# Block-sparse query and key rows: one product each and a spread by transfers, instead of one product for each place

## What is computed

```python
q = jax.nn.relu(jnp.einsum('btd,nde->btne', x, encoder_query))   # 8 heads of 16
v = jax.nn.relu(jnp.einsum('btd,nde->btne', x, encoder_value))
...                              # metric: softplus of a small network on the mean of q
for h in range(NH):
    kw = q_h[:, idx, :]                       # the 64 tokens up to this one
    diff = kw - q_h[:, :, None, :]
    dist = jnp.sqrt((diff * diff * metric).sum(-1) + 1e-08)
    neg, loc = jax.lax.top_k(-dist, k_act)    # 32 nearest
    infl = jnp.exp(-topd) / sum
    context = sum over the nearest of infl * v, plus a gated term of q_h
    outs.append(q_h * context)
```

## Time and profile before

| | |
|---|---|
| median of 3 runs | 2972.43 us (2961.26 to 2973.3) |
| the profiled execution | 2964.93 us, span of its instructions 2963.2 us |
| granted TensorE clock, mean | 0.921 of full speed |
| instructions | 60847 |
| DMA | 84.79 MB, mean 29 GB/s |

### The profile page before, as it was taken

One profiled execution on the slowest core, in us unless ns is written; L12 is line 12 of the kernel. 1 busy time (PEld: TensorE's weight loads), 2 busy tenths in 40 slices (PEclk: granted clock), 3 DMA queues, 4 the chain that ended last, 5 costly groups with the idle time before them and its releaser, 6 DMA issues.

```text
span 2963.2 us, 60847 instructions
## 1 busy us (share of the span) xinstructions
PE 2411.7 (81%) x21171; PEld 1048.0 (35%) x21171; DVE 2112.0 (71%) x10282; ACT 2263.2 (76%) x3151; POOL 688.7 (23%) x869
## 2 busy tenths in 40 slices
PE   4788778888788887988888897888888888887666
PEld 1112242244332443334432443324433344224444
DVE  5801778957797668966789577876689667982695
ACT  4798668977699677987689776996779877994432
POOL 3020115111251114401152112511134011311331
PEclk6599789999899999999889998999999999999887
DMA  3011001100011001210011000110012000000000
GB/s 87 30 46 43 2 19 48 50 18 6 23 56 43 17 8 28 65 31 9 20 44 54 18 6 23 54 42 17 6 35 65 31 9 12 14 17 1 17 20 11
DMA packets 98518, 84.79 MB, mean 29 GB/s; under 512 B 19954, under 2 KB 79540, under 8 KB 98212
## 3 DMA queue, kind: packets, MB, share of 16 engines
q1 hardware_dynamic: 97968, 80.41, 9.2%
q10 hardware_dynamic: 244, 0.49, 0.1%
HBM read 55.32 MB, written 25.44 MB: 27 GB/s over the span
## 4 chain that ended last, share of the span: by engine, by line
ACT 34%; PE 33%; DVE 19%; issue 6%; POOL 5%; SPq 2%; DMA 0%; ACTq 0%; DVEq 0%; POOLq 0%
PE banks L802 30%; ACT PT L1141 17%; DVE xn L1473 4%; ACT pq L1128 4%; DVE h L1476 3%; DVE pq L1260 2%; ACT xn L1086 2%; ACT hparts L1152 2%; POOL Aop L781 2%; PE banks L809 2%; ACT h L1153 2%; ACT h L1054 1%; DVE h L1458 1%; ACT Bs L1054 1%; POOL qkf L728 1%
## 5 line engine op out<-in xcount | busy, mean ns | idle before, releaser
L1141 ACT ACTIVATE PT<-banks 128x1024 f32<-128x1024 f32 x1024 | 996.6, 1038 | 47.4 <-PE banks L802 44.7
L1260 DVE CUSTOM_DVE_ANT_0 pq<-pq,banks 128x512 f32<-128x512 f32 x1024 | 653.4, 683 | 175.5 <-ACT pq L1128 174.8
L1128 ACT ACTIVATE pq<-banks 128x1024 f32<-128x1024 f32 x512 | 523.2, 1023 | 223.5 <-PE banks L802 198.1
L802 PE MATMUL banks<-PT,Vg 128*9 128x512 f32 x4096 | 545.9, 605 | 2.3 <-ACT PT L1141 2.3
L802 PE MATMUL banks<-Q,K 51*128 51x512 bf16 x2048 | 391.0, 393 | 139.9 <-ACT PT L1141 113.3
L802 PE MATMUL banks<-K,Q 48*128 48x512 bf16 x2048 | 360.9, 431 | 80.6 <-ACT pq L1128 37.2
L762 POOL TENSOR_TENSOR hparts<-h,hparts 128x512 fp32r<-128x512 f32 x112 | 140.5, 1272 | 1009.2 <-ACT h L1153 1009.2
L1473 DVE MATCH_REPLACE8 xn<-h,xn 128x96 f32<-128x96 f32 x1536 | 352.2, 241 | 0.0
L802 PE MATMUL banks<-hparts,W 128*128 128x512 f32 x1024 | 303.9, 426 | 39.6 <-ACT h L1153 27.8
L802 PEld LDWEIGHTS banks<-Q,K 51*128 51x128 bf16 x2048 | 96.2, 93 | 620.4 <-ACT PT L1141 534.9
L1476 DVE MAX8 h<-xn 128x8 f32<-128x96 f32 x1536 | 263.0, 243 | 0.0
(11 more groups left out here) (207 smaller groups left out, 3256.3 us busy)
## 6 DMA issues: line engine op xcount, KB each, us to landing
Vw<-scratch_v SPq DMA_DIRECT2D x256, 51.0 KB, 2.1
scratch_k<-pq SPq DMA_DIRECT2D x24, 384.0 KB, 3.1
K<-scratch_k SPq DMA_DIRECT2D x126, 72.0 KB
qkf<-in_hidden_states SPq DMA_DIRECT2D x16, 512.0 KB, 4.4
scratch_q<-pq SPq DMA_DIRECT2D x24, 256.0 KB, 2.3
Q<-scratch_q SPq DMA_DIRECT2D x126, 48.0 KB
K<-scratch_k SPq DMA_DIRECT2D x126, 48.0 KB
scratch_v<-Bs SPq DMA_DIRECT2D x8, 544.0 KB, 3.5
```

The lines of the kernel that those rows point to most:

```text
L802: return pe.matmul(o, l, r, start=start, stop=stop)
L1128: act.activation(cut(g), ring_pair if work is TURN0 and g % 2 else pair[0], ACT.Relu).then_inc(diff_out.sem, 1)
L1141: act.activation(PT[:, at:at + 2, :], pair[g % ESLOTS], ACT.Exp, scale=1.0 if i % 8 < 4 else -1.0).then_inc(probs.sem, 1)
L1260: dve.tensor_tensor_reduce(r, r, pair[1 + g % 2][:, par, :], 1.0, -3.0e38, ALU.subtract, ALU.max, mred[:, par, i, qt:qt + 1]).then_inc(max ...
```

## The change

- eqd and the places' order change: in qd and B the linear copies of four heads fill partitions 0 to 63, the squared copies 64 to 127. The masks half0, half1 and the loads of w2d and rows follow (27 loads instead of 31 at the start).
- "qd" loses its four products. SyncE, once "he" is evicted and the last Aop of the batch before is made, copies qh's 64 rows of each half to both places of qd: four DMAs.
- "key" is two products of xrev with eq into kh (a new name for a part of h2); "pad" is a copy of 64 columns on VectorE; at "spread" SyncE copies kh's rows to B by four DMAs. GpSimd waits for the first four at "aop" 0, VectorE for the others at "keys".
- "qtok" is eight transposes of qh instead of eight products.
- The exponential and logarithm of the metric and VectorE's operations behind them move to "an", and "an" moves behind "qtok".
- xrev is no longer continued by 64 columns.
- The slots and weights of P are new, and since the number of ring uses is now odd, each turn has its own list with its own bank numbers.

The diff, cut to its core:

```diff
-USES = dict(..., he=1, qd=1, hid=1, mod=1, key=1, pad=1, an=1, ...)
+USES = dict(..., he=1, hid=1, mod=1, key=1, an=1, ...)
-WEIGHTS P, from "flip" on: 0.90, 2.00, 2.00, 1.00, 1.31, 1.00, 1.94, 2.00, 2.00, 0.48, 2.00, 2.21, 0.55, 1.10, 1.10, 1.11, 1.11
+WEIGHTS P, from "flip" on: 0.90, 2.00, 1.94, 2.00, 1.00, 1.00, 2.00, 1.00, 2.21, 0.55, 1.10, 1.10, 1.11, 1.11
-SLOTS_P += [(1, [("flip", 0), ("flip", 1)]), (2, [("he", 0), ("he", 1)]), (2, [("qd", 0), ("qd", 1)]), (1, [("hid", 0), ("ev", 0)]),
-            (1, [("qd", 2)]), (1, [("mod", 0)]), (1, [("qd", 3)]), (2, [("key", 0), ("key", 1)]), (2, [("key", 2), ("key", 3)]),
-            (1, [("pad", 0), ("an", 0)]), (2, [("qtok", 0), ("qtok", 1)]), (4, [("keys", 0)]),
-            (1, [("gate", 0)]), (2, [("hebb", 0), ("hebb", 1)]), (2, [("aop", 0)]), (2, [("dist", 0)]), (2, [("dev", 0)])]
+SLOTS_P += [(1, [("flip", 0), ("flip", 1)]), (2, [("he", 0), ("he", 1)]), (1, [("qd", 0)]), (2, [("key", 0), ("key", 1)]),
+            (1, [("spread", 0), ("hid", 0), ("ev", 0)]), (1, [("mod", 0)]), (2, [("qtok", 0), ("qtok", 1)]), (1, [("an", 0)]),
+            (4, [("keys", 0)]), (1, [("gate", 0)]), (2, [("hebb", 0), ("hebb", 1)]), (2, [("aop", 0)]),
+            (2, [("dist", 0)]), (2, [("dev", 0)])]
...
 SyncE
+            def spread(to, rows, sem):
+                for f in range(2):
+                    for half in range(2):
+                        sp.dma_start(to[64 * half:64 * half + 64, f, :], rows[64 * f:64 * f + 64, :]).then_inc(sem.sem, 16)
...
+                    if stage == "qd":
+                        for i in range(2):
+                            sp.wait_ge(*R.moved(c, use["he", i]))
+                        sp.wait_ge(*aop_p.at(b, 0))
+                        spread(qd, qh, qd_in)
+                    if stage == "spread":
+                        for i in range(2):
+                            sp.wait_ge(*R.moved(c, use["key", i]))
+                        sp.wait_ge(*kpad.at(b, 1))
+                        spread(B, kh, b_in)
...
 TensorE
-                    if stage == "qd":
-                        h = n % 2
-                        one(c, k, [(R.bank(k)[:, :], eqd[:, n // 2, :], xT[:, HALF * h:HALF * h + HALF], True, True)])
                     if stage == "key":
-                        h = n % 2
                         if n == 0:
                             pe.wait_ge(*R.made(c, k, use["flip", 0], use["flip", 1]))
-                        one(c, k, [(R.bank(k)[:, :], eqd[:, n // 2, :], xrev[:, HALF * h:HALF * h + HALF], True, True)])
-                    if stage == "pad":
...
+                        one(c, k, [(R.bank(k)[:, :], eq[:, :], xrev[:, HALF * n:HALF * n + HALF], True, True)])
                     if stage == "qtok":
-                        one(c, k, [(R.bank(k)[:, P * q:P * q + P], xT[:, P * (4 * n + q):P * (4 * n + q) + P],
-                                       eq[:, :], True, True) for q in range(4)])
+                        pe.wait_ge(*R.free(c, k))
+                        for q in range(4):
+                            ins = pe.transpose(R.bank(k)[:, P * q:P * q + P], qh[:, P * (4 * n + q):P * (4 * n + q) + P], ident[:, :])
+                        ins.then_inc(R.ready.sem, 1)
...
 ScalarE
-                    if stage == "key" and n == 0:
+                    if stage == "key":
+                        evict(c, k, kh[:, HALF * n:HALF * n + HALF], R.bank(k)[:, :], ACT.Relu)
+                    if stage == "an":
                         act.wait_ge(*met_z.at(b, 1))
                         act.activation(met[:, 3, :], met[:, 2, :], ACT.Exp, scale=-1.0).then_inc(met_e.sem, 1)
                         act.wait_ge(*met_e.at(b, 1))
                         act.activation(met[:, 4, :], met[:, 3, :], ACT.Ln, bias=1.0).then_inc(met_l.sem, 1)
-                    if stage in ("qd", "key"):
...
 VectorE
-                        dve.wait_ge(*R.moved(c, use["flip", 1]))
-                        dve.tensor_copy(xrev[:, T:RPAD], xrev[:, T - 1:T].broadcast_to([P, WIN])).then_inc(xpad.sem, 1)
...
-                    if (stage, n) == ("key", 3):
+                    if stage == "spread":
+                        dve.wait_ge(*R.moved(c, use["key", 1]))
+                        dve.tensor_copy(kh[:, T:RPAD], kh[:, T - 1:T].broadcast_to([P, WIN])).then_inc(kpad.sem, 1)
+                    if stage == "an":
                         dve.wait_ge(*met_l.at(b, 1))
...
-                        dve.wait_ge(*R.moved(c, use["key", 3]))
-                        dve.wait_ge(*R.moved(c, use["pad", 0]))
+                        dve.wait_ge(*b_in.at(b, 1))
                         dve.wait_ge(*v_out.at(b, 2))
```

More of the change, by code:

```diff
@@ L61 @@
 PT_SLOTS = 4
-USES = dict(qk=4, v=1, turn=1, back=1, wo=1, mturn=1, lnT=1, lnTa=2, fa=1, fb=1, fc=1, flip=1, he=1, qd=1, hid=1, mod=1,
-            key=1, pad=1, an=1, qtok=1, hebb=1, dist=2, ev=2, wt=2, pv=1, st=1, dec=1)
+USES = dict(qk=4, v=1, turn=1, back=1, wo=1, mturn=1, lnT=1, lnTa=2, fa=1, fb=1, fc=1, flip=1, he=1, hid=1, mod=1,
+            key=1, an=1, qtok=1, hebb=1, dist=2, ev=2, wt=2, pv=1, st=1, dec=1)
 def uses(stage, n):
@@ L230 @@
 FIRST, FIRST_USE, _k = numbered(HEAD, 0)
-TURN0, TURN0_USE, _k0 = numbered(phases(True, False, False), _k)
-NR = sum(uses(stage, n) for _, stage, n in phases(True, True, True))
-TURN1, TURN1_USE, _k1 = numbered(phases(True, True, False), _k0 - NR)
-TURN, TURN_USE, _ = numbered(phases(True, True, True), _k1 - NR)
-TURN7, TURN7_USE, _k7 = numbered(phases(False, True, True), _k1 - NR)
-LAST, LAST_USE, _ = numbered(TAIL, _k7)
-assert NR % 2 == 0
+TURN0, TURN0_USE, _k = numbered(phases(True, False, False), _k)
+TURN1, TURN1_USE, _k = numbered(phases(True, True, False), _k)
+TURNS = []
+for _c in range(2, NB - 1):
+    _work, _use, _k = numbered(phases(True, True, True), _k)
+    TURNS.append((_work, _use))
+TURN7, TURN7_USE, _k = numbered(phases(False, True, True), _k)
+LAST, LAST_USE, _ = numbered(TAIL, _k)
 class Count:
@@ L254, with __init__ @@
 class Ring:
-    def __init__(self, banks, sem, name, uses):
+    def __init__(self, banks, sem, name):
         self.banks = banks
-        self.ready = Count(sem(f"{name}_ready"), uses)
-        self.evicted = [Count(sem(f"{name}_evicted{i}"), uses // 2) for i in range(2)]
+        self.ready = Count(sem(f"{name}_ready"), 0)
+        self.evicted = [Count(sem(f"{name}_evicted{i}"), 0) for i in range(2)]
     def bank(self, k):
@@ L453, in hybrid_block_kernel @@
         ln_q = count("ln_q", 2)
-        xpad = count("first_repeated", 1)
+        kpad = count("first_key_repeated", 1)
+        qd_in = count("query_rows_spread", 1, 4 * 16)
+        b_in = count("key_rows_spread", 1, 4 * 16)
         met_z = count("metric_in", 1)
@@ L1181, in go @@
                     if stage == "qtok":
[L1182 removed]
+                        evict(c, k, qtok[:, 4 * n:4 * n + 4, :], rows_of(R.bank(k), P))
                     if stage == "gate":
```

40 lines of the change are left out of this document (13 added, 27 removed).

## The result

| | before | after |
|---|---|---|
| median of four runs each | 2968.5 us (2961.3 to 2973.3) | 3001.9 us (2998.8 to 3007.0) |
| ratio, 95% interval | | 1.011 (1.0094 to 1.0126) |
| span of the profiled execution | 2963.2 us | 3005.3 us |
| granted TensorE clock, mean | 0.921 | 0.904 |

The predicted 2973 us is 29 us too low, and the time lies 2 us outside the range. The profiled executions are 42 us apart, the medians 33 us: the one of after is the slowest of its four, the one of before lies 4 us under its median.

What follows compares the result with a forecast made beforehand. No engine full; VectorE's order was taken to decide the stretch from "he" to "dist". Per turn +2.7 - 1.2 = +1.5 us, seven turns +10.5, tail -2.8: +7.7 on 2964.9, forecast 2973 us, range 2933 to 3000.

Steps and rivals of the forecast that it cites:

- rival B: TensorE at its lower clock from "qtok" to "dist", slowing "hebb" and distance products: +2.5 us a turn, 2993 us; chance 0.24.
- The order slides by two groups: New weights put "flip" after 54 row-maximum groups instead of 52, with 8 instead of 10 between "he" and "dist".
- Ahead of "he", +2.7 us: Two more groups ahead of the encoder products: one among the feed-forward products, one ahead of the normalization; +2.7 us a turn.
- Its part for the normalization: One added group behind "fcd", ahead of the normalization on VectorE's full queue: two cut maxima, +1.3 us a turn.
- The part for the feed-forward products: One added group there turns one cut distance of 1.71 us into two of 1.56: +1.4 us a turn.
- The clock, nothing in the sum: TensorE's granted clock from "an" on had no term in the sum; its lower level was left to rival B.
- From "he" to the first distance, -1.2 us: Walk from "he" to the first distance eviction: about 31.9 us instead of 33.1, most of TensorE's saving becoming idle time.
- The metric's wait at "an": TensorE waits for VectorE's metric ahead of the "an" products, 2 to 3 us, no longer covered by key products.
- The transfers, nothing: Query and key row copies, 2.1 MB a batch, cost nothing: covered by 3.7 us or more ahead of "keys".
- Rival C: Rows arrive late: at twice the transfer time +3.5 us a turn and +3 in the tail, 3003 us; chance 0.08.
- The tail, -2.8 us: Tail without groups: "mod" gains 1.1 us, "an" follows two short transposes, so "keys" comes 2.8 us sooner.
- TensorE's busy time, -71 us: Removed "qd", key and "qtok" products take 8.9 us of TensorE a batch, 71 us in all.

Runs made afterwards that it cites:

- e12_one: Kernel before, all products kept, P's weights lowered half way (sum 79.04), so one group more stands ahead of "he": 2981.2 us, 1.0047.
- e2_slide: Kernel before, all products kept, only P's weights lowered (sum 76.65) to give the changed kernel's order up to "he": 2999.6 us, 1.0097.
- e1_order: Changed kernel with P's last weights raised (sum 81.44), restoring the order of before ahead of "he": 2977.1 us, 1.0022.
- e3_busy2: Changed kernel plus six unused 512-column products a batch, two ahead of the "an" wait, four at "gate": 2979.7 us, 1.0033.
- e9_ordmet: Changed kernel with the order of before ahead of "he" and the metric's steps moved from "an" to "qtok": 2960.3 us, 0.9973.
- e4_metric: Changed kernel with the metric's exponential and logarithm moved to the first "qtok", VectorE's operations to the second: 2990.6 us, 1.0071.
- e7_double: Changed kernel with each spread preceded in its queue by the same four transfers into DRAM: 3035.3 us, 1.0225.

## Why the prediction was wrong, step by step

Two terms of the sum failed: the price ahead of "he", which was too low, and the clock from "an" on, which stood in the sum with nothing and was left to rival B.

- *The order slides by two groups: right.* *Ahead of "he", +2.7 us: too low by 1.9 us a turn* (4.55). Its part for the normalization held: +4.9 at "he" in the turn shown less 3.8 at the last "fcd" leaves 1.1 against 1.3. The part for the feed-forward products, +1.4 by the distance of two cuts, measured 3.8. I had priced one added group; e12_one shows 3.6 us without one. In turn 1, without side "q", "he" comes 9.1 us later, and I had given turn 1 the price of the others; e2_slide has 5.8 of it, and the other 3.3 us are open. With the order of before, 25 us of the loss are gone (e1_order).
- *The clock, nothing in the sum: wrong; rival B had the mechanism.* "hebb" takes 3.78 us instead of 2.05 (rival: 3.2), the first distances 1.61 instead of 1.53 (rival: 2.8). With TensorE kept busy by unused products "hebb" is back at 2.05 us and 22 us are gone (e3_busy2). It doesn't take the missing products: e2_slide has them all and the same 3.78 us in every turn. The 25 and the 22 us can't be added up, as the order moves the clock too.
- *From "he" to the first distance, -1.2 us: the size came out on the mean (-1.4; -0.5 in the turn that I had walked through), the reason did not.* e2_slide wins the same 1.4 us with all products in place. What their removal was to give went into the metric's wait and the clock: in the order of before, moving the metric gives 15 to 17 us (e9_ordmet against e1_order).
- *The metric's wait at "an": right.* Forecast 2 to 3 us, measured 2.0. It was in the sum, but as harmless; moved out, it gives 11 us (e4_metric), and 15 to 17 in the order of before (e9_ordmet).
- *The transfers, nothing: right in the turns, with 2.2 us of cover instead of 3.7.* SyncE took 0.8 us for each issue, not 0.4, and they landed in 4.2 and 4.7 us, as the rows below show. In the turn shown the query rows are there 10.1 us behind "he" (forecast 9.5), the key rows at 15.9 (15), the store at 18.0 (18); keys asked at 20.5 instead of 21.7. Rival C at twice the time was priced at 3.5 us a turn; e7_double, with twice the bytes, measured some 3.6 us (355.0 against 351.4) in turns 3 to 6 and 7 us in turn 2.
- *The tail, -2.8 us: wrong, +7.1.* Both its parts failed: keys wait for the store, and the clock stays down for 30.7 us. The tails with all products take 212.4 us (before), 214.0 (e2_slide) and 216.5 (e12_one), so 3 to 7 us belong to the change itself.
- *The exponent stage, nothing: wrong, +1.2 us a turn.*
- *TensorE's busy time, -71 us: wrong, -25.* The products went (76 us); the slower "hebb" and "an" took 22 us back, and other groups 29.

The sum as it came out, where I had 1.5 us for each of seven turns and -2.8: 4.55 - 1.5 + 0.4 + 1.2 = 4.6 us in each of turns 2 to 6 (0.4 between the first distance and the first exponential; the -1.5 is of these five turns), 8.8 in turn 1, 3.6 in turn 7 and 7.1 in the tail: 42 us.

## What to carry to other kernels

Where one list orders all engines, an edit that changes the weights behind a point also moves every step ahead of it: run the kernel before with the new weights alone before you judge the edit, and don't price a shift by counting groups. And look at the clock of the kernel with the new weights as well: here the order alone put "hebb" at the lower level. The products taken off TensorE gave nothing as long as the wait that they had covered stayed (the metric's, 15 to 17 us). With that moved and the order of before, the change pays, though "hebb" still runs at the lower level (29.7 us in e9_ordmet). Taken together, the change with the order of before and the metric made early is 0.3 to 0.4% faster than the kernel before; as it was made it is 1.1% slower.

## What the runs showed of the hardware

DMA issues of the changed kernel by tile, beside the earlier trace rows (count, size of one, us to landing):

```profile
B<-h SPq DMA_DIRECT2D x32, 272.0 KB, 4.7
...
qd<-qh SPq DMA_DIRECT2D x32, 256.0 KB, 4.2
scratch_q<-pq SPq DMA_DIRECT2D x24, 256.0 KB, 2.5
...
scratch_v<-Bs SPq DMA_DIRECT2D x8, 544.0 KB, 5.1
```

256 KB from 64 partitions to 64 land in 4.2 us (the first of each four in 2.9 to 3.1), where the 256 KB stores to DRAM that were there before (scratch_q) take 2.5; the store behind them takes 5.1 us instead of 3.5. The Trainium skill's page "SBUF — State Buffer", "Door 1: The DMA port swizzle", has 64 partitions reach half of the ports; the trace agrees in direction, but four of them were in flight at once, and no run here has one alone. In e7_double the same 256 KB from 64 partitions into DRAM, again four in flight, take 4.0 us, so a target of 64 partitions isn't needed for it. What the prediction had worked out from half the rate came close: the key rows there near 16 us (15.9 in the turn shown) and the store 2 us late in the tail (1.7). Beyond that I hadn't expected that a kernel gets 22 us faster by six products that nobody reads (e3_busy2), nor that the lower clock would last 30.7 us in one piece in the tail, in a stretch in which TensorE is busy 37.7 of 60 us.
